# Three attention layers on one core: counts in five pieces, another way to the target rows, and GpSimd's addition in two instructions of 400

## The reference

```python
xs = (h @ Ws).reshape(N, H, C)
alpha_s = jnp.sum(xs * a_s, axis=-1)          # per source node and head
alpha_d = jnp.sum(xd * a_d, axis=-1)          # per target node and head
e = jax.nn.leaky_relu(alpha_s[src] + alpha_d[dst], 0.2)
ex = jnp.exp(e - jax.ops.segment_max(e, dst, num_segments=N)[dst])
alpha = ex / (jax.ops.segment_sum(ex, dst, num_segments=N)[dst] + EPS)
out = jax.ops.segment_sum(xs[src] * alpha[:, :, None], dst, num_segments=N)
```

## Time and profile before

| | us |
|---|---|
| median of 3 runs | 4754.59 (4748.15 to 4755.33) |
| the profiled execution | 4748.57 |
| its span | 4746.7 |
| DVE busy | 3664.5 (77%) |
| PE busy | 3341.2 (70%) |
| ACT busy | 3213.9 (68%) |
| POOL busy | 1872.2 (39%) |

### The profile page before, as it was taken

The page is one execution under the profiler, slowest core; times in us unless marked ns, Lnnn a source line. Parts: engine busy times, 40 slices in busy tenths (PEclk is TensorE's granted clock), DMA queues, the critical chain, the costliest instruction groups (busy, mean ns, idle before and its releaser), DMA issues.

```text
span 4746.7 us, 68862 instructions
## 1 busy us (share of the span) xinstructions
PE 3341.2 (70%) x20934; PEld 1593.7 (34%) x20934; DVE 3664.5 (77%) x8187; ACT 3213.9 (68%) x7531; POOL 1872.2 (39%) x1368
## 2 busy tenths in 40 slices
PE   6999888655555555555555555555699999958799
PEld 3444345211111121111112111111476777735444
DVE  8999978688889969889996988999677777764211
ACT  5888711688888868888886888888566676754100
POOL 0000031344444524444542444445377777761000
PEclk8999987788888878888887888888799999978899
DMA  4444474011112111111211112120377777661665
GB/s 156 158 155 155 154 278 149 21 44 62 48 44 65 44 44 44 48 63 44 65 44 44 44 44 66 44 65 1 102 237 237 237 241 237 232 219 37 242 239 208
DMA packets 387514, 552.88 MB, mean 116 GB/s; under 512 B 23781, under 2 KB 358021, under 8 KB 386922
## 3 DMA queue, kind: packets, MB, share of 16 engines
q1 hardware_dynamic: 358114, 494.48, 29.9%
q0 software_dynamic: 23024, 48.93, 3.9%
q10 hardware_dynamic: 6040, 5.35, 0.4%
HBM read 352.81 MB, written 195.86 MB: 116 GB/s over the span
## 4 chain that ended last, share of the span: by engine, by line
DVE 45%; PE 17%; ACT 10%; DMA 7%; issue 6%; POOL 2%; SPq 1%; DVEq 0%; ACTq 0%; POOLq 0%
DVE big L1897 11%; DVE big L1905 11%; DVE pick L1905 11%; PE quad L1139 7%; DMA src_bc<-pe_src_d 4%; DVE big L2020 3%; ACT quad L914 2%; DMA big<-table_d,src_win 2%; POOL big L752 2%; PE psL L1296 2%; PE psZ L1299 2%; PE quad L1471 1%; DVE lane_x L1911 1%; ACT hT L1007 1%; ACT pick L905 1%
## 5 line engine op out<-in xcount | busy, mean ns | idle before, releaser
L735 POOL TENSOR_TENSOR pick<-pick,big 128x800 f32<-128x800 f32 x600 | 1132.9, 1888 | 1413.0 <-ACT pick L905 1413.0
L1296 PE MATMUL psL<-pick,big 128*32 128x400 f32 x2400 | 620.0, 600 | 898.2 <-DVE big L1905 897.8
L914 ACT ACTIVATE quad<-big,keep 128x400 f32<-128x400 f32 x1200 | 674.2, 582 | 188.1 <-DVE big L1897 188.0
L1905 DVE SCALAR_TENSOR_TENSOR big<-quad,big 128x400 f32<-128x400 f32 x1200 | 660.2, 570 | 161.5 <-ACT quad L914 150.9
L905 ACT ACTIVATE pick<-big,keep 128x400 f32<-128x400 f32 x1200 | 737.4, 615 | 66.9 <-PE psZ L1299 66.4
L752 POOL DMA_INDIRECT big<-table_d,src_win x672 | 643.3, 957 | 275.7 <-issue 187.7
L1905 DVE SCALAR_TENSOR_TENSOR pick<-quad,big 128x400 f32<-128x400 f32 x1200 | 682.9, 569 | 67.1 <-ACT quad L914 64.3
L914 ACT ACTIVATE quad<-pick,keep 128x400 f32<-128x400 f32 x1200 | 702.3, 585 | 5.9 <-POOL pick L735 5.9
L1296 PE MATMUL psL<-big 128*32 128x400 f32 x2400 | 619.7, 600 | 0.0
L1299 PE MATMUL psZ<-pick,ones 128*32 128x400 f32 x2400 | 588.9, 573 | 0.0
L1299 PE MATMUL psZ<-big,ones 128*32 128x400 f32 x2400 | 588.5, 573 | 0.0
(11 more groups left out here) (366 smaller groups left out, 6761.3 us busy)
## 6 DMA issues: line engine op xcount, KB each, us to landing
big<-A_d SPq DMA_DIRECT2D x17, 6400.0 KB, 19.7
rows_d<-big SPq DMA_DIRECT2D x112, 896.0 KB
A_d<-big SPq DMA_DIRECT2D x396, 200.0 KB, 1.9
big<-A_d SPq DMA_DIRECT2D x24, 2600.0 KB, 9.8
big<-A_d SPq DMA_DIRECT2D x24, 2400.0 KB, 9.8
big<-A_d SPq DMA_DIRECT2D x32, 1600.0 KB, 11.5
big<-table_d,src_win POOLq DMA_INDIRECT x672
src_bc<-pe_src_d SPq DMA_DIRECT2D x56, 64.0 KB, 6.1
```

The lines of the kernel that those rows point to most:

```text
L735: pool.tensor_tensor(soft_2[n % A_SLOTS], soft_2[n % A_SLOTS], row_2[J % 2], ALU.add).then_inc(bent_p, 1)
L914: nc.scalar.activation(bank(n, h), soft(n, h), ACT.Exp, bias=s_all[:, 2, n % NT, h:h + 1]).then_inc(soft_rdy, 1)
L1296: nc.tensor.matmul(acc[0][C * h:C * h + C, 0:CH], xs_1[:, t, C * h:C * h + C], soft(n, h), start=(t == 0), stop=(t == NT - 1))
L1905: v.scalar_tensor_tensor(soft(n, h).rearrange("p (b w) -> p b w", w=W), bank(n, h).rearrange("p (b w) -> p b w", w=W), CAP, a, ALU.min, AL ...
```

## The change

- POOL adds the row to head 0 and to head 1 in an instruction of 400 each, and each waits for its own head alone (`half_done`). `half_a` counts both heads.
- The share's multiply moves from DVE (`divide`, now `invert`, the reciprocal alone) to POOL (`shares`, after tile 4, and at the end of a layer).
- The row of a chunk: `own_rows`, `own_row`, `middle_part` and `cut_row` are gone. `top_rows` is three float32 products accumulated in PSUM (the targets' own score, a constant, the highest levels) which give both values that `near` needs, so `near` has two operations. `spread_row` and `keep_row` multiply its float32 result directly (4 rows instead of 96 bfloat16 rows). Constants `of_top`, `of_low`, `of_own`, `to_all`, `to_near`, `ones_row`, `of_eps` are float32.
- The order: rows are spread 0, 1, 3, 2 at t = 19 to 22 and copied by ACT at t = 21, 22, 23 and 24; `keep_row` 1 at t = 22 and 0 at 23; levels three a tile in tiles 3 to 7, five at t = 11 and five at 15; `top_rows` and `highest` at t = 17; `totals` inside tile 1, in front of exponent(n,0); `layer_rows` at t = 7.
- Counts come in five pieces of five tiles (rows of 80 values instead of 208 or 192) into a ring of eight, with four semaphores.
- Head of a layer: one product of 132 columns for each tile of xs, three tiles to a bank, copied by ACT in two operations for three tiles; `settle` writes the levels in five pieces, each with its own semaphore counts towards ACT and PE; its four small operations on `ends_4` are replaced by six on `ends_s`, `of_top` and `of_low`.

```diff
-SPLIT = 13
-RING = 3
+PIECE = 5
+RING = 8
+PIECE_SEMS = 4
+    ROWS_IN = (0, 1, 3, 2)
+    NX = -(-NT // 3)
+    PIECES_FIRST = (1, 2, 4, 6, 8)
+    PIECES_LAST = (3, 5, 7, 9, 10)
...
+        def half_done(n, h):
+            g, k = divmod(n, NT * NCH)
+            return 2 * NT * NCH * g + ((k + 1 if k < 2 else 2 * k) if h == 0 else min(2 * k + 3, 2 * NT * NCH))
...
+        def piece_in(k):
+            return 16 * (k // PIECE_SEMS + 1 + (k % PIECE_SEMS < PARTS - 1))
...
-                for late in range(2):
-                    k = 2 * J + late
+                for i in range(PIECES):
+                    k = PIECES * J + i
                     if k >= RING:
                         sp.wait_ge(ring_used, k - RING + 1)
-                    q = (NT - SPLIT) * W if late else HALF_W
-                    sp.dma_start(a_half[k % RING][:, :, 0:q], A_d[a:a + CHB, :, HALF_W * late:HALF_W * late + q].rearrange("b p q -> p b q")
-                                 ).then_inc(a_part[k % RING], 16)
+                    if k >= PIECE_SEMS:
+                        sp.wait_ge(a_part[k % PIECE_SEMS], piece_in(k - PIECE_SEMS))
+                    sp.dma_start(a_half[k % RING], A_d[a:a + CHB, :, PIECE_W * i:PIECE_W * (i + 1)].rearrange("b p q -> p b q")
+                                 ).then_inc(a_part[k % PIECE_SEMS], 16)
...
+            def shares(J):
+                pool.wait_ge(totals_rdy, 2 * J + 2)
+                pool.tensor_tensor(share, share, total_b, ALU.mult).then_inc(share_rdy, 1)
...
-                pool.wait_ge(half_a, n + 1)
-                pool.tensor_tensor(soft_2[n % A_SLOTS], soft_2[n % A_SLOTS], row_2[J % 2],
-                                   ALU.add).then_inc(bent_p, 1)
+                for h in range(2):
+                    pool.wait_ge(half_a, half_done(n, h))
+                    pool.tensor_tensor(soft(n, h), soft(n, h), row_2[J % 2][:, CH * h:CH * h + CH], ALU.add).then_inc(bent_p, 1)
+                if J % NCH and t == 4:
+                    shares(J - 1)
+                if J % NCH == NCH - 1 and t == NT - 1:
+                    shares(J)
...
+                        if c and t == 1:
+                            totals(J - 1)
                         exponent(n, 0)
...
                         exponent(n, 2)
-                        if c and t == 1:
-                            totals(J - 1)
-                        if c and t == 6:
+                        if c and t == 7:
                             layer_rows(g, J - 1)
                         if c < NCH - 1:
-                            if t == 3:
-                                own_row(J + 1)
-                            if t == 20:
-                                middle_part(J + 1)
-                            if t == 21 or t == 22:
-                                near_row(J + 1, t - 21)
+                            if 21 <= t < 23:
+                                near_row(J + 1, ROWS_IN[t - 21])
                             if t == 23:
+                                near_row(J + 1, 3)
+                            if t == 24:
                                 near_row(J + 1, 2)
-                                near_row(J + 1, 3)
...
-            def top_rows(J):
+            def top_rows(g, J):
                 pe.wait_ge(near_rdy, 2 * J + 1)
-                nc.tensor.matmul(psR[0:H, :], of_head, bits, start=True, stop=True).then_inc(lev_ps, 1)
+                to = psR[0:TW_ROWS, :]
+                nc.tensor.matmul(to, of_own[:, g, :], feat[g % 2][:, CH * (J % NCH):CH * (J % NCH + 1)], start=True, stop=False)
+                nc.tensor.matmul(to, of_low[0:1, :], ones_row[0:1, :], start=False, stop=False)
+                nc.tensor.matmul(to, of_top, bits, start=False, stop=True).then_inc(lev_ps, 1)
...
-                nc.tensor.matmul(psR, to_all[0:96, h, :], parts[J % 2][0:96, :], start=True, stop=True).then_inc(row_ps, 1)
+                nc.tensor.matmul(psR, to_all[:, h, :], v_4, start=True, stop=True).then_inc(row_ps, 1)
...
-                    nc.tensor.matmul(psY[t % 2][:, 0:D], feat[g % 2][:, P * t:P * t + P], w_att[:, g, 0:D], start=True, stop=True)
-                    nc.tensor.matmul(psH[:, H * t:H * t + H], feat[g % 2][:, P * t:P * t + P], w_att[:, g, D:D + H],
-                                     start=True, stop=True).then_inc(xs_ps, 1)
+                    ins = nc.tensor.matmul(psY[k % 2][:, (t % 3) * (D + H):(t % 3 + 1) * (D + H)], feat[g % 2][:, P * t:P * t + P],
+                                           w_att[:, g, 0:D + H], start=True, stop=True)
+                    if t % 3 == 2 or t == NT - 1:
+                        ins.then_inc(xs_ps, 1)
...
-                            if 3 <= t < 16:
-                                levels(g, J + 1, t - 3, t - 2)
-                            if t == 16 or t == 17:
-                                levels(g, J + 1, SPLIT + 6 * (t - 16), SPLIT + 6 * (t - 15))
-                            if t == 18:
-                                top_rows(J + 1)
-                            if 20 <= t < 23:
-                                spread_row(J + 1, t - 20)
+                            if 3 <= t < 8:
+                                levels(g, J + 1, 3 * t - 9, 3 * t - 6)
+                            if t == 11:
+                                levels(g, J + 1, 15, 20)
+                            if t == 15:
+                                levels(g, J + 1, 20, 25)
+                            if t == 17:
+                                top_rows(g, J + 1)
+                            if 19 <= t < 23:
+                                spread_row(J + 1, ROWS_IN[t - 19])
+                            if t == 22:
+                                keep_row(J + 1, 1)
...
+                for i in range(PIECES + 1):
+                    if i < PIECES:
+                        at = lev[:, PIECE * i:PIECE * (i + 1), :, :]
...
+                        v.tensor_scalar(at, at, 0.0, 1.0, ALU.max, ALU.min).then_inc(lev_rdy, 1)
+                    if i:
+                        at = lev[:, PIECE * (i - 1):PIECE * i, :, :]
+                        dve.wait_ge(lev_in, PIECES * g + i)
+                        v.tensor_scalar(at, at, -1.0, None, ALU.add).then_inc(lev_rdy, 1)
...
-                link(v.tensor_scalar(m_4, psR[0:H, :], ends_4[:, 3:4], ends_4[:, 5:6], ALU.mult, ALU.add))
-                link(v.tensor_tensor(v_4, m_4, own_4, ALU.add))
-                link(v.tensor_scalar(v_4, v_4, 0.0, NEG_SLOPE * DEEPEST, ALU.max, ALU.min))
-                link(v.tensor_tensor(v_4, v_4, m_4, ALU.subtract))
+                link(v.tensor_scalar(m_4, psR[32:32 + H, :], 0.0, NEG_SLOPE * DEEPEST, ALU.max, ALU.min))
+                v.tensor_tensor(v_4, m_4, psR[0:H, :], ALU.subtract).then_inc(near_rdy, 1)
...
-            def divide(J):
-                dve.wait_ge(totals_rdy, J + 1)
-                link(v.reciprocal(total_b, total_b))
-                v.tensor_tensor(share, share, total_b, ALU.mult).then_inc(share_rdy, 1)
+            def invert(J):
+                dve.wait_ge(totals_rdy, 2 * J + 1)
+                v.reciprocal(total_b, total_b).then_inc(totals_rdy, 1)
```

199 lines of the change are left out of this document (91 added, 108 removed).

## The result

The changed kernel takes 4469.45 us (median of 4 runs, 4461.63 to 4479.53) against 4754.13 for the kernel before: a ratio of 0.9405, 95% interval 0.9381 to 0.9428. The forecast was 4445 us, range 4385 to 4570. The profiled execution took 4463.87 us, its span 4462.0, which is 284.7 less than the profiled execution of before; the sum had said 307.

A forecast was written before the change was run, and what follows sets the result against it. ACT was taken as the bound, DVE close behind. Savings of 12.6 us for 21 chunks (265), 3 for last chunks, 41 for heads, less 2, sum to 307: 4748.6 - 307 = 4441.6, plus 3, said as 4445 us, range 4385 to 4570.

The forecast's parts named there:

- What bounds the kernel, ACT with DVE close behind: Steady tiles: ACT's six steps take 3.11 to 3.12 us a tile and set the pace; DVE needs 3.01 when fed.
- Two additions of 400 (0.9): Tile loop: POOL's split addition, about 1050 ns each, leaves ACT's 3.115 us a tile, saving 0.9 us a chunk.
- Near rows without the split (4.45): `near` and `cut_row`: DVE's eight dependent operations become two, 1.3 us for 5.83; ACT's wait falls, saving 4.45 us a chunk.
- Order of the rows (2.7): Chunk's end: giving each row copy its own tile removes 2.7 of 2.9 us of ACT's waits for row products.
- totals (2.0): Chunk's start: copying totals earlier in tile 1 cuts ACT's wait for PE's sums from 3.0 to 0.9, saving 2.0 us.
- share (1.6): Behind the reciprocal: moving the share's multiply to POOL leaves DVE 2.67 of 4.27 us, saving 1.6 us a chunk.
- Second count, 86.2 us for the chunk: Chunk counted from ACT's work, 81.5 us, plus remaining stalls, 4.7 us: 86.2 us, a saving of 12.8.
- The half-clock tile (0.4): Tiles 3 to 7: three levels a tile on PE make one tile late at half clock, charged 0.4 us a chunk.
- the PE rival: Row stretch: PE's clock stays low with float32 rows, 5.6 us a chunk come back, 4563 us in all; chance 0.2.
- Heads (13.8 each): Head of a layer: fused products, levels in pieces and shorter rows save 13.8 us, 41 over three layers.
- Five pieces: Count loads: landing in 4 to 10 us stays hidden; DVE's extra waits to free pieces cost 0.3 us a chunk.
- The short-row rival: Count loads: short rows cost more than long ones, so the transfer queue sets the chunk and the kernel is slower; chance 0.05.

The follow-up runs named there:

- e4_share_dve: The changed kernel with the multiply of share and reciprocal back on DVE, directly behind the reciprocal: 4503.82 us, ratio 0.9472 to the kernel before.
- e3_split_alone: The kernel before with only POOL's addition split into two of 400, each waiting for its own head: 4740.43 us, ratio 0.9965.
- e6_near_block: The changed kernel with four more chained DVE clamps of the same 4 x 400 row inside `near`: 4530.55 us, ratio 0.9515 to the kernel before.

## Why the prediction was right, and where it was not

**What bounds the kernel, ACT with DVE close behind.** Right. Tiles went to 3.11 to 3.12, which is ACT's six steps of 0.52, and not to DVE's 3.01.

**Two additions of 400 (0.9).** Right: 1037 ns each where 1050 was put, and 1.0 back when undone. The 1.2 when done alone holds another gain, which comes next.

**Near rows without the split (4.45).** Its basis is shown, a chained block passes through whole (3.06 gave 3.1). `near` takes 1.1 us (2494.03 to 2495.12), 0.2 less than put. I did not run the bfloat16 split itself in the changed kernel.

What the prediction did not see is that a part of the DVE blocks that it counted was waiting for POOL. Operations of DVE that overlapped an addition of POOL ran long (number of runs; ns min, median, max); the first two rows are of the kernel before (a step of `near`, and the share's multiply), the third is the same multiply in e4_share_dve:

```profile
L1879 DVE TENSOR_TENSOR Z<-Z,lane_x x24: 562/2122/2132, 876.5 to 3217.8; 4x400 f32<-4x400 f32 x24
L1912 DVE TENSOR_TENSOR sm<-sm,lane_x x24: 575/1669/1676, 998.7 to 3334.4; 128x400 f32<-128x400 f32 x24
L1928 DVE TENSOR_TENSOR sm<-sm,lane_x x24: 574/574/575, 971.4 to 3097.4; 128x400 f32<-128x400 f32 x24
```

In the kernel before, three of each 24 met no addition of POOL and took 0.56 to 0.58 us; the other 21 began inside an addition of 800 and ended 0.43 us after it. So 1.56 of the 5.83 us of the near block and 1.1 of the 1.67 of the multiply were POOL's. With additions of 400 in e3_split_alone they take 1.28 and 0.83 (medians), which is the second gain there. In the changed kernel `near` reads PSUM in both operations and takes 0.57 and 0.56. The totals of the prediction stand, as it took the durations from the rows; what they consist of does not. The added block of e6_near_block is half of this kind too: two of its clamps take 0.36, two 1.17 and 1.07.

**Order of the rows (2.7), totals (2.0), share (1.6).** That these waits went is shown by the profile: those for row products are gone, 3.2 for PE's sums became 0.8, and 8.9 for DVE 3.4. What each term is worth is shown only in part. Undone singly, the mean period rises by 1.1 to 1.5 (order), 2.9 to 3.2 (totals) and 2.4 to 2.8 us (share), and in each a part is PE at the lower clock for longer. For the order 1.0 is its own wait, and the rest can't be told from the clock. For the totals 2.1 is the copy's place, the size that the prediction gave it, and 0.9 and more is the clock. The share's run gives 0.7 at an equal clock, but it puts back a multiply of 0.57 and not the one of 1.67, so it does not test the 1.6. I did not undo two at once, so whether the terms add is not shown either.

**Second count, 86.2 us for the chunk.** Exact for 11 of 18. Its stalls were 4.7; the profile has 3.4 + 0.8.

**The half-clock tile (0.4).** This is the step that was wrong. I argued that the clock would stay up in the row stretch, as PE's idle time before its fall (7.29 us) would go. The idle time went, to 1.9 us at most ahead of a long fall, and the clock fell nonetheless, in every chunk for at least 3.4 us and in five of 18 for 16. The fall was nothing new: in the kernel before each of the 18 chunks has 8.9 to 22.6 us at the lower clock in the same window, yet those with 8.9 and most of those with 15.8 take the same 98.9. There PE's slow products cost next to nothing; with DVE's and the rows' waits gone and float32 rows on PE, the next chunk waits for them. A chunk with the long fall costs 4.9 us, near the 5.6 of the PE rival. The rival was right on the mechanism and price in part of the chunks, where I had given it a chance of 0.2 for all of them or none. In the sum: 5 x 4.9 = 24.5 us, and the observed 18 chunks stand 18 x (12.6 - 11.45) = 20.7 below the forecast, nearly the whole miss of 22.3. The layers' first chunks, which the 18 periods leave out, have it too, with a granted clock of 0.87, 0.69 and 0.50 in this window in the three layers. The third's, 34 to 8 us ahead of its first reciprocal:

```profile
2406.42:2432.42 26.00, 24.19 (x100) 6.21 (x96) 18.59 (x36) 21.28 (x42) 12.00 (x12) 0.50 0.17 41
```

From the first half bend to that reciprocal 104.5 us pass, 110.6 before: 6.1 saved where about 11 were due. (The low end of the range is 4389 by the sum's own bounds, not 4385, a slip that changes nothing.)

**Heads (13.8 each).** Too low by 4, which hid that last loss. The fused products save 13.7 us (2300.50 to 2309.11, against 2502.2 to 2524.47), not 10: a fused step is 0.32 (8.05 over 25), less than either case that I had weighed. Settling and levels save 5.2 (5.3 forecast), and what follows costs 1.2 more than before (2.4 forecast).

**Five pieces.** Hidden, as said. A piece lands in 5.7 us, just above the 4 to 5 at which only bytes count, and pieces of half that row length in 6.8. The rule of the Trainium skill (DMA: Bandwidth & Descriptors, Specifications), that rows under 512 bytes fall short of line rate, agrees in direction with what the queue shows: with the same 494.5 MB its share of the 16 engines went from 34.6% to 42.0% with twice the rows, (0.420 x 4467.1 - 0.346 x 4462.0) x 16 / 386000 = 14 ns of an engine for each further row. Whether the limit lies at 512 no run here shows. The short-row rival needed 17.2 us a piece and had no weight here.
